# Last attention stage: rows of the previous expert layer fetched one duo per step instead of in a burst

## The reference, cut to what matters

```
# third block, expert layer: every token takes 2 of 8 experts
topk_expert_outputs = take_along_axis(expert_outputs, gather_idx, axis=2)
mixed_output = sum(topk_expert_outputs * topk_weights[..., None], axis=2)
x = x + mixed_output
# fourth block, attention: 16 heads of 8 channels over 64 keys
xn = layernorm(x)
attn = softmax(einsum('bhqc,bhkc->bhqk', q(xn), k(ctx)) * SCALE)
x = x + (einsum('bhqk,bhkc->bhqc', attn, v(ctx)) @ o_w.T + o_b)
# then its own expert layer (router, 2 of 8 experts, and a shared expert)
```

## Time and profile before

| what | value |
|---|---|
| device time, median of 3 runs | 1499.96 us |
| lowest and highest run | 1497.4 and 1508.93 us |
| span of the profiled execution | 1589.0 us |
| of it the attention stage of this change | about 1098 to 1380 us of the span |
| busy over the span | PE 84%, PEld 71%, DVE 64%, ACT 56%, POOL 36% |

### The profile page before, as it was taken

How to read it: one execution, slowest core, us unless ns; L and a number is a source line. 1 busy time by engine, 2 the same in 40 slices (tenths; PEclk the granted TensorE clock), 3 DMA queues, 4 the chain that set the end, 5 groups by cost and what they waited for, 6 DMA issues and landing times. The chain is left out here.

```text
span 1589.0 us, 43573 instructions
## 1 busy us (share of the span) xinstructions
PE 1336.9 (84%) x17143; PEld 1126.5 (71%) x17143; DVE 1013.3 (64%) x2619; ACT 890.4 (56%) x2064; POOL 569.6 (36%) x553
## 2 busy tenths in 40 slices
PE   7999999989999979972799749997377787878884
PEld 5888999867888968861455528996156576768784
DVE  7798997845344339979678784553467676543335
ACT  4666666534444449976466335663145555326674
POOL 3344334310000013323566316662723424254552
PEclk8999999999999999985999888999577878799997
DMA  6511100099980003400000102221101100012225
GB/s 191 180 33 28 39 20 3 3 140 146 175 101 1 1 19 118 125 9 0 25 19 16 55 6 61 71 71 57 48 25 31 39 27 27 19 45 74 75 69 177
DMA packets 148825, 94.13 MB, mean 59 GB/s; under 512 B 56240, under 2 KB 136624, under 8 KB 148112
## 3 DMA queue, kind: packets, MB, share of 16 engines
q1 hardware_dynamic: 139984, 73.51, 21.5%
q0 software_dynamic: 8640, 17.84, 3.7%
HBM read 51.32 MB, written 39.99 MB: 57 GB/s over the span
## 5 line engine op out<-in xcount | busy, mean ns | idle before, releaser
L1756 POOL DMA_INDIRECT moe_x_rows<-moe_rows,moe_source x71 | 87.3, 1230 | 92.3 <-DVE moe_source L1848 51.5
L439 POOL TENSOR_TENSOR wide_probs<-wide_probs,wide_key_mask 128x512 f32<-128x512 f32 x44 | 64.5, 1486 | 119.8 <-ACT wide_probs L623 119.8
L2464 DVE TENSOR_TENSOR moe_hidden<-banks,moe_gate 128x256 f32<-128x256 f32 x103 | 43.2, 424 | 89.8 <-ACT moe_gate L2661 62.7
L919 POOL TENSOR_TENSOR attn_col_bd<-attn_col_t,group_mask_sb 128x1024 f32<-128x1024 f32 x32 | 60.6, 1895 | 104.9 <-ACT attn_row_t L1150 104.9
L2273 POOL DMA_INDIRECT moe_results<-moe_y_rows,moe_until_blocks x71 | 68.8, 968 | 73.5 <-DVE moe_y_rows L2476 51.2
L889 POOL MEMSET attn_v_bd<- 128x576 f32 x2 | 1.2, 614 | 250.8 <-POOLq L168 250.8
L2076 POOL DMA_INDIRECT moe_rows<-moe_xhat,moe_slot x64 | 62.2, 972 | 66.8 <-DVE moe_slot L2401 48.7
L2661 ACT ACTIVATE moe_gate<-banks 128x256 f32<-128x256 f32 x103 | 40.2, 393 | 72.3 <-PE banks L2885 59.2
L2885 PE MATMUL banks<-moe_xb_t,moe_until_blocks 128*128 128x128 f32 x568 | 76.9, 279 | 0.1
L3280 ACT ACTIVATE moe_router<-banks,moe_rb_sb 128x512 f32<-128x512 f32 x64 | 41.4, 689 | 63.1 <-PE banks L3413 45.4
L2226 POOL DMA_INDIRECT moe_until_blocks<-moe_results,moe_slot x64 | 60.9, 952 | 43.5 <-POOLq L168 25.4
(11 more groups left out here) (464 smaller groups left out, 4380.1 us busy)
## 6 DMA issues: line engine op xcount, KB each, us to landing
moe_rows<-route_empty_sb SPq DMA_DIRECT2D x8, 2624.0 KB, 22.8
attn_ctx<-in_ctx_t SPq DMA_DIRECT2D x48, 128.0 KB, 2.1
moe_until_blocks<-moe_rows SPq DMA_DIRECT2D x71, 66.0 KB
moe_pack_sb<-in_moe_pack SPq DMA_DIRECT2D x8, 578.0 KB, 4.2
moe_results<-moe_y_rows SPq DMA_DIRECT2D x71, 64.0 KB, 1.5
moe_w_sb<-in_moe_w SPq DMA_DIRECT2D x2, 2048.0 KB, 7.2
moe_until_back<-moe_results SPq DMA_DIRECT2D x16, 256.0 KB, 6.0
moe_pack_sb<-in_moe_pack SPq DMA_DIRECT2D x9, 384.0 KB, 5.1
```

What stands on the lines that cost most here:

```text
L439: nc.gpsimd.tensor_tensor(some, some, keys, ALU.mult).then_inc(masked, 1)
L919: nc.gpsimd.tensor_tensor(col_bd[:], col_t[u.parity][:].unsqueeze(1).to_broadcast(shape), w["group_mask"][:].unsqueeze(2).to_broadcast(sha ...
L1756: nc.gpsimd.indirect_dma_start(x_rows[b % GATHERS][:], None, rows, bass.IndirectOffsetOnAxis(ap=source[:, b:b + 1], axis=0)).then_inc(gath ...
```

## The change

The five constants are new, and the gather moves within GpSimd's loop. Before the loop no duo but 0 to 2 is fetched. In step `s` of the loop GpSimd first waits until PE has transposed duo `s-1` (`xt_made` at `s`, from step 1 on), fetches duo `3+s`, and only then makes `based` of duo `s-3`. The DVE adds one duo per step from duo 6 on (two before in steps 4 and 6, and none later than step 11; now up to step 13), and the 16 duos are normed in 11 parts instead of 8.

```diff
-BACK_AHEAD = 8
-BACK_PARTS = [range(0, 1), range(1, 2), range(2, 3), range(3, 4), range(4, 6), range(6, 8), range(8, 12), range(12, 16)]
-BACK_AT = {2: [3], 3: [4, 5], 4: [6, 7], 5: [8], 6: [9, 10], 7: [11], 8: [12], 9: [13], 10: [14], 11: [15]}
-BACK_LINKS = {2: 3, 3: 4, 5: 5, 7: 6, 11: 7}
+BACK_AHEAD = 3
+BACK_PARTS = [range(0, 1), range(1, 2), range(2, 3), range(3, 4), range(4, 5), range(5, 7), range(7, 9), range(9, 11), range(11, 13),
+              range(13, 14), range(14, 16)]
+BACK_AT = {2: [3], 3: [4, 5], 4: [6], 5: [7], 6: [8], 7: [9], 8: [10], 9: [11], 10: [12], 11: [13], 12: [14], 13: [15]}
+BACK_LINKS = {2: 3, 3: 4, 4: 5, 6: 6, 8: 7, 10: 8, 12: 9, 13: 10}
...
-                for duo in range(3, BACK_AHEAD):
-                    if duo in (4, 6):
-                        pool.wait_ge(xt_made, duo // 2 - 1)
-                    bring_back(duo)
                 pool.wait_ge(core.cleared, 2 * CLEARS * DMA_INC)
                 pool.wait_ge(const_ready, 1)
                 for s in range(STEPS_ALL):
                     c = s - 3
+                    if BACK_AHEAD + s < DUOS:
+                        if s >= 1:
+                            pool.wait_ge(xt_made, s)
+                        bring_back(BACK_AHEAD + s)
                     if inside(c):
                         if c >= 2:
                             pool.wait_ge(added, c - 1)
                         pool.wait_ge(back_both, c + 1)
                         nc.gpsimd.tensor_tensor(based[c % 2][:], pair(core.x, c), constant[:].unsqueeze(1).to_broadcast([P, 2, P]),
                                                 ALU.add).then_inc(based_ready, 1)
-                        if BACK_AHEAD + c < DUOS:
-                            bring_back(BACK_AHEAD + c)
                     if s >= 10:
                         g, k = (s - 10) // 2, s % 2
                         d.send(core, pool, g, k, 2 * g + 1)
```

## The result

The changed kernel took 1513.05 us in the median of six runs (1501.08 to 1515.37), the kernel before 1498.06 us in the same comparison (1496.44 to 1508.93). The two medians lie 15 us apart, but the runs spread over as much, so the ratio of all runs is used here: 1.0081, with an interval from 1.0054 to 1.0107. Measured again, beside other kernels, it was 1.0072 (1.0047 to 1.0097). So the change costs 11 to 12 us by the ratios. The forecast was 1496 us in a range from 1480 to 1510, and it was wrong in sign.

The account below looks back on a forecast made before the run. PE was taken to lead with the DVE close behind, step 3's scores crawling beside GpSimd's gathers. Profiled sum -19.6 + 1.4 + 1.4 = -16.8 us; for the runs -6.5 + 2.8 = -3.7, so 1496 us, range 1480 to 1510.

Parts of the forecast that it names:

- the 95 us without a name: Chain of the profiled execution: 6% of 1589 us as "issue" and "another core or an unknown queue", set beside 89 us.
- the crawl: Step 3's 32 score matmuls on PE, 20.77 us instead of 1.12 during GpSimd's gathers; 19.6 us to go if gathers cause it.
- The burst: Start of the stage: later gathers wait for the third transpose; -19.6 us in the profile, -6.5 in runs; 9.04 us wait stays.
- no link: Rival: the scores stay slow without gathers, or gathers stay because `xt_made` 3 comes early; 1503 us, chance 0.15.
- Norm parts: DVE, eleven parts instead of eight: 9.9 us of new DVE time, mostly covered by waits; +1.4 us, bounds 0 and +9.9.
- the DVE is the bound: Rival: without stalls PE's steps and the DVE's waits shrink, leaving three parts uncovered, +9.9 us; 1510 us, chance 0.10.
- The step 11 term: DVE in step 11, which loses the norm part of eight tiles: -1.3 us.
- Step 12 (+0.7) and step 13 (+2.0): DVE steps that each get a duo and a part, against waits of 2.24 and 0.26 us plus 2.01 us of scores.
- More steps with gathers: Steps 3 to 12 fetch a duo instead of 4 to 9; four more at 0.35 us, +1.4 us.
- GpSimd falls behind: Rival: in steps 10 to 12 GpSimd's step passes 13.7 us and `based` is late; 1516 us, chance 0.05.
- Contention: DVE additions beside GpSimd: no term, since two take 0.60 us in step 10, GpSimd issuing, and in step 11, idle.
- my 12 us: Rival of the shared GpSimd and VectorE interface: ten duos meeting gathers cost 1.2 us each; 1508 us, chance 0.03.

Follow-up runs that it names:

- base: The kernel before, unchanged, run again for a second profile (span 1500.7 us); 1501.71 us median of ten, ratio 1.0015.
- before_plus3: The kernel before with three more norm parts, on tiles 28 to 31, in steps 6, 8 and 10; 1506.20 us, ratio 1.0040.
- after_minus3: The changed kernel without the arithmetic of three of its eleven norm parts (steps 8, 10 and 12); 1504.49 us, ratio 1.0033.
- norm_only: The kernel before, its gathers kept, with the change's tables of additions, norm parts and links; 1509.39 us, ratio 1.0067.
- norm_only_minus3: Gathers of the kernel before, tables of the change, without the arithmetic of three norm parts (steps 8, 10 and 12); 1500.70 us, ratio 0.9998.
- after: The changed kernel, in its first profile (span 1504.0 us); 1513.05 us median of six, ratio 1.0081 to the kernel before.
- before_minus3: The kernel before without the arithmetic of three of its eight norm parts (steps 5, 7 and 11); 1493.84 us, ratio 0.9963.
- based_behind: The kernel before with one move, each step's gathers issued ahead of `based` on GpSimd; 1506.61 us, ratio 1.0062.

## Why the prediction was wrong

**The yardstick.** The step that failed first is the reading of the profiled execution as the kernel's own, only stretched. I had set its 89 us over the runs beside the 95 us without a name, and then discounted one item of it, the crawl, while all other rows were taken at face value. From line 2524 of step 4 to that of step 19 that execution took 204 us (1175.4 to 1379.0), base 169; up to step 4, where the crawl and the 9.04 us wait lie, it took 24 us more, and behind step 19 another 25 (210.0 against 184.7). So every wait that I used as cover, the 3.27 us of step 8 and the 2.24 of step 12, came from an execution with a granted clock of 0.79 instead of 0.88 (the same two values from step 4 to step 19). In base the wait at the end of step 8 is 1.38 us, and at the end of step 10 there is none.

**The burst: -6.5 us predicted for the runs, none shown** (-1.4 between single profiles, 49.18 against 47.76, inside what kernels differ there whatever their burst). There was no crawl to end. That GpSimd would not wait at 1134 because the third transpose comes early was written under "no link", and is what happened. That rival's time, 1503 us, was still too low, because its other term was.

**Norm parts: +1.4 us predicted, about +6 to +10 measured.** This is the term that decided. Three parts by themselves cost 6.0 us (before_plus3), 5.9 (after_minus3), and 10 by the pair norm_only and norm_only_minus3 (1.0067 - 0.9998 = 0.69%, an estimate across two chips). In the profile the whole term, steps 4 to 14, came to 7.15 us. The prediction's own upper bound was +9.9. Its rival "the DVE is the bound" named the mechanism, the reason (in a run without stalls PE's steps shrink and the waits with them) and 1510 us, and got 0.10. I had counted each part against a wait in one even step. With a part added in steps 6, 8 and 10 of the kernel before, the waits of base there (1.38 us and none) were gone, and the time rose all the same. That a part also costs where the next step's PE then waits for the DVE is my reading, not shown by itself. The step 11 term (-1.3) has the right sign: that stretch fell from 13.97 to 12.24 us. Step 12 (+0.7) and step 13 (+2.0) were +2.7 each: in step 12 the wait was even longer than read, 2.64 us, but the DVE got 5.34 us more work instead of 5.0, and the wait and the 2.01 us of scores did not both cover it. Step 13 keeps its +2.7 with three parts left out elsewhere (norm_only_minus3), so it does not come from those three but from what step 13 itself got, a duo and a part.

**More steps with gathers (+1.4), and additions in steps 12 and 13.** No run takes the gathers alone into more steps. after_minus3 differs from norm_only_minus3 by them and by the place of `based`, and stands 0.35% higher in the runs and 2.2 us later at step 14; how much of that is the gathers' own stays open. Without the three parts the later additions cost nothing on balance (0.9998).

**GpSimd's queue: nothing predicted, nothing seen as a queue.** The sends of step 10 begin at 1219.71 in after; by step 14 GpSimd waits 8.63 us for slots again, and the tail is equal to 0.1 us. "GpSimd falls behind" did not happen.

**Contention: no term predicted, 0 to 5 us measured.** Of the two equal rows of 0.60 us one had a DMA issue of GpSimd beside it and one nothing, and DMA issues do not lengthen additions. What does is `based` right behind a DMA issue, which the change itself brings about; I had moved `based` behind four gathers and looked only at whether it would be late. The move alone costs 0.62% in the kernel before (1.0045 to 1.0079). In the change I can only bracket it: with the parts left out the gathers' side costs 0.33% (1.0013 to 1.0052), with them 0.05 to 0.14%, below what can be told apart. That the two effects don't add is plausible, since a later `based` then falls into gaps elsewhere, but it wasn't tested. The Trainium skill, "Trainium Architecture — The Big Picture", section "What this means for kernel authors", calls the pair of ports that VectorE and GpSimd share "an exclusive lock (not a bandwidth split)". The held instruction of 1.16 us agrees with that, and shows that a price in proportion to the instruction's own length, as I had worked out my 12 us, is the wrong form.

**What stays open.** Why the first profiled execution was 89 us slow; why the changed kernel, 5.7 and 6.5 us behind base at step 14 in its two profiles, loses 11 to 12 in the runs; and why DVE time taken away in a profile by 10.9 us at step 14 (before_minus3) is worth 5.5 us in the runs. For both of the latter the granted clock is the candidate. Of the changed kernel's two profiles, equal to 0.7 us up to step 14, one then ran its steps 14 to 16 at 0.81 and 0.74, the other at 1.00 and 0.85, and was 10 us ahead at step 19 (234.9 against 224.7). Over 91 runs of the kernel before, time and granted clock go together with a correlation of -0.79, 9.2 us for 0.01 of clock. Which of the two leads is not shown.

## What to carry to other kernels

Before a wait is used as cover, see that the profiled execution's time is near the median of the runs; if it is not, its steps, waits and stalls all belong to another kernel than the one that is timed, and one item of it can't be discounted alone. A chain of short instructions added to an engine that is busy over 0.8 of the time has to be priced at most of its own length, also where the engine seems to wait: here about 2 us in the runs for each norm part of some 2.5 us of DVE time (7.6 us for three in before_plus3). The reverse did not hold as well: leaving three parts out gave 5.5 us back, but a regrouping into seven gave nothing. So splitting a batch of normalizations to fit a smoother transfer schedule must be paid for by the transfers, which were hidden. When a step is moved on GpSimd, ask besides "is it late" which DVE instruction it will meet.

## What the runs showed of the hardware

A GpSimd tensor instruction (0.73 us) issued directly behind an indirect DMA holds DVE instructions with operands in SBUF that begin up to some 0.6 us ahead of it or beside it: 0.15 us became 1.16 in based_behind, and in after two in a row took 0.68 and 0.61 instead of 0.16. A memset of GpSimd does the same, and `based` itself is longer where additions began just ahead of it, 0.88 us at 1244.56. The DVE in after, an instruction of one input that takes 0.17 us elsewhere, while two such memsets run on GpSimd from 1108.84 to 1109.95:

```profile
1108.46 1.51 DVE L218 TENSOR_SCALAR norm_half<-norm_var 128x2 uint32<-128x2 uint32 x1
```

The DVE's subtractions of maxima, which read PSUM, were not lengthened by `based` (2.35 us for two in base with it beside, and in based_behind without). The gathers and sends by themselves (0.94 to 1.0 us each) leave additions and small TENSOR_TENSOR instructions alone: in all 15 profiles none of two or four elements that began inside one, with no tensor instruction of GpSimd behind it, took over 0.20 us. A small TENSOR_SCALAR is another matter: each one that began 0.25 to 0.4 us ahead of the end of such a gather or send lasted until about that end, and none did that began over 0.46 us ahead. Base, 0.42 us instead of 0.17, and the gather beside it, 1.03 us instead of 0.94:

```profile
1188.45 0.42 DVE L2306 TENSOR_SCALAR norm_var<-norm_var 128x4 f32<-128x4 f32 x1
```

```profile
1187.84 1.03 POOL L2226 DMA_INDIRECT moe_until_blocks<-moe_results,moe_slot  x1 [0.30 <-issue]
```

The granted clock of PE, whose two levels are 1.2 and 2.4 GHz, was between 0.58 and 1.00 in one and the same stretch of 121 matmuls, which then took 15.54 or 10.43 us.
